# q's rotation in three engines instead of one: crosswise copies on ScalarE, the sine multiply on GpSimd

## The reference, cut to what matters

```
h = take(weight, ids)                                  # (8, 512, 256)
x = layernorm(h)
q, k, v = x @ w_aq, x @ w_ak, x @ w_av                 # 8 heads of 128
q, k = rope(q), rope(k)   # even*cos - odd*sin | even*sin + odd*cos over the halves of a head
s = q @ k.T / 128, causal;  p = softmax(s);  o = p @ v
h = h + o @ w_ao
h = h + moe(layernorm(h))                              # 8 experts, 1024 tokens each
```

## Time and profile before

| what | value |
|---|---|
| median of 3 runs | 1285.78 us (1285.78 to 1285.96) |
| the profiled execution: time, span | 1286.61 us, 1284.8 us |
| mean granted TensorE clock in it | 0.957 |
| busy: PE, DVE, ACT, POOL | 1148.5, 912.1, 609.5, 740.8 us |

### The profile page before, as it was taken

The page is one execution under the profiler, slowest core; times in us unless marked ns, Lnnn a source line. Parts: engine busy times, 40 slices in busy tenths (PEclk is TensorE's granted clock), DMA queues, the critical chain, the costliest instruction groups (busy, mean ns, idle before and its releaser), DMA issues. The chain is left out here.

```text
span 1284.8 us, 21944 instructions
## 1 busy us (share of the span) xinstructions
PE 1148.5 (89%) x7255; PEld 985.3 (77%) x7255; DVE 912.1 (71%) x1980; ACT 609.5 (47%) x1306; POOL 740.8 (58%) x783
## 2 busy tenths in 40 slices
PE   3899999999999999999999978015999999999995
PEld 2688888878878878878888863004999999999994
DVE  5888888898888998988988853775555555553522
ACT  4455545545555445545555543102654654655541
POOL 3776676776766776766766730005654744744425
PEclk9999999999999999999999998556999999999998
DMA  5000100100100100100100001304423623624212
GB/s 184 5 14 1 38 30 0 37 29 0 41 24 0 41 24 9 43 13 33 33 1 34 17 2 34 106 0 133 116 34 99 133 34 99 132 34 99 34 17 33
DMA packets 42170, 57.60 MB, mean 45 GB/s; under 512 B 8896, under 2 KB 34944, under 8 KB 41984
## 3 DMA queue, kind: packets, MB, share of 16 engines
q0 software_dynamic: 13824, 21.24, 9.2%
q1 hardware_dynamic: 28288, 35.58, 8.3%
HBM read 35.71 MB, written 16.91 MB: 41 GB/s over the span
## 5 line engine op out<-in xcount | busy, mean ns | idle before, releaser
L1125 DVE TENSOR_TENSOR hT_lo<-hid,hT_hi 128x512 fp32r<-128x512 f32 x128 | 89.4, 699 | 178.8 <-ACT hT_hi L1243 178.8
L268 ACT ACTIVATE prob<-bank,row_min 128x512 f32<-128x512 f32 (+3 forms) x256 | 136.1, 532 | 113.1 <-DVE row_min L389 113.0
L199 POOL TENSOR_SCALAR prob<-prob,row_inv 128x512 f32<-128x512 f32 (+3 forms) x256 | 135.0, 540 | 68.2 <-DVE row_inv L393 66.7
L1241 ACT ACTIVATE hid<-up,b_e 128x512 f32<-128x512 f32 x128 | 88.1, 688 | 154.8 <-PE up L1308 143.6
L339 DVE TENSOR_TENSOR pT_lo<-bank,pT_hi 128x384 fp32r<-128x384 f32 (+1 forms) x192 | 114.2, 595 | 50.8 <-ACT pT_hi L248 50.6
L949 POOL DMA_INDIRECT got<-routed_rows,tokens x64 | 85.8, 1341 | 102.7 <-DVE tokens L1119 85.4
L212 POOL TENSOR_TENSOR kT_lo<-k_cos,kT_hi 128x512 fp32r<-128x512 f32 x64 | 84.2, 1315 | 78.1 <-ACT kT_hi L248 78.1
L248 ACT ACTIVATE oT_hi<-bank 128x512 fp32r<-128x512 f32 x64 | 38.4, 599 | 186.5 <-PE bank L519 178.5
L206 POOL TENSOR_TENSOR q_cos<-q_cos,q_sin 128x512 f32<-128x512 f32 x64 | 82.3, 1287 | 55.1 <-DVE q_sin L376 55.0
L969 POOL DMA_INDIRECT out<-y,tokens x64 | 103.2, 1613 | 17.3 <-issue 14.8
L389 DVE TENSOR_REDUCE row_min<-bank 128x1 f32<-128x512 f32 (+3 forms) x256 | 112.4, 480 | 0.2
(11 more groups left out here) (196 smaller groups left out, 3855.8 us busy)
## 6 DMA issues: line engine op xcount, KB each, us to landing
raw<-in_w SPq DMA_DIRECT2D x16, 1024.0 KB, 8.1
emb_res<-emb SPq DMA_DIRECT2D x8, 512.0 KB, 3.7
out<-h SPq DMA_DIRECT2D x8, 512.0 KB, 2.9
routed_rows<-x SPq DMA_DIRECT2D x8, 512.0 KB
x<-in_wq SPq DMA_DIRECT2D x1, 1024.0 KB, 5.3
x<-in_wk SPq DMA_DIRECT2D x1, 1024.0 KB, 5.0
x<-in_wv SPq DMA_DIRECT2D x1, 1024.0 KB, 7.2
x<-in_wo SPq DMA_DIRECT2D x1, 1024.0 KB, 10.0
```

What stands on the lines that cost most here:

```text
L199: nc.gpsimd.tensor_scalar(pr, pr, row_inv[:, h % 2, k:k + 1], 1.0, ALU.mult, ALU.mult).then_inc(s["norm_done"], 1)
L268: nc.scalar.activation(prob[:, h % 2, col:col + w], s_ps[bk][:, pc:pc + w], ACT.Exp, bias=row_min[:, h % 2, k:k + 1], scale=-1.0, accum_ou ...
L1125: nc.vector.tensor_tensor(out, in_, hi.bitcast(F32), ALU.subtract)\
L1241: nc.scalar.activation(hid[:, t % 2, :], up_ps[t % 2][:], ACT.Gelu, bias=bias)
```

## The change

Three edits, all in attention:

1. For q, VectorE keeps only the cosine multiply (`mul_q`). ScalarE copies the two halves of the projection crosswise from PSUM into `q_sin` (`swap`), at the head of its slot, and GpSimd multiplies `q_sin` by the sine table before its add. Whatever waited for `q_rope` on TensorE now waits for `q_swap`. k's rotation stays.
2. On ScalarE, `qT_hi` moves behind `pT_hi` 0; on GpSimd, the add for k moves ahead of the low part of q.
3. In the start, the rounding of the output weight (`wo_hi`, 128x2048) moves from before slot 0 to slot 0, behind `kT_hi`.

```diff
             def add(b, h, x):
                 n = b * H + h
-                cos, sin = (q_cos, q_sin) if x == "q" else (k_cos, k_sin)
-                after(pool, f"{x}_rope", n + 1)
+                if x == "q":
+                    cos, sin = q_cos, q_sin
+                    after(pool, "q_swap", n + 1)
+                    nc.gpsimd.tensor_tensor(sin[:], sin[:], rope_q[:, 1, :], ALU.mult)\
+                        .then_inc(s["q_sin"], 1)
+                    after(pool, "q_sin", n + 1)
+                else:
+                    cos, sin = k_cos, k_sin
+                    after(pool, "k_rope", n + 1)
                 nc.gpsimd.tensor_tensor(cos[:], cos[:], sin[:], ALU.add).then_inc(s[f"{x}_add"], 1)
...
                     if live:
+                        add(b, h, "k")
                         low(b, h, "q")
-                        add(b, h, "k")
                         low(b, h, "k")
...
+            def swap(b, h):
+                n = b * H + h
+                after(act, "q_mul", n + 1)
+                after(act, "q_add", n)
+                nc.scalar.activation(q_sin[0:64, :], proj_ps[0][64:128, :], ACT.Copy)
+                nc.scalar.activation(q_sin[64:128, :], proj_ps[0][0:64, :], ACT.Copy)\
+                    .then_inc(s["q_swap"], 1)
...
-            act.wait_ge(s["wo_in"], 16)
-            hi_of(w_o[0][:], wraw_o, "w_hi")
...
+                    if live:
+                        swap(b, h)
                     if ok(h - 3):
                         after(act, "o_done", n - 3 + 1)
                         after(act, "out_done", n - 3)
                         hi_of(oT[0][:], o_ps[:], "o_hi")
+                    if ok(h - 2):
+                        t_high(b, h - 2, 0)
                     if live:
                         qk_high(b, h, "q")
-                    if ok(h - 2):
-                        t_high(b, h - 2, 0)
                     if ok(h - 1):
                         exp(b, h - 1, 0)
...
                     if live:
                         qk_high(b, h, "k")
+                    if isinstance(b, int) and b == 0 and h == 0:
+                        act.wait_ge(s["wo_in"], 16)
+                        hi_of(w_o[0][:], wraw_o, "w_hi")
...
-            def rope(b, h, x):
...
+            def mul_q(b, h):
+                n = b * H + h
+                after(dve, "q_proj", n + 1)
+                after(dve, "q_lo", n)
+                nc.vector.tensor_tensor(q_cos[:], proj_ps[0][:], rope_q[:, 0, :], ALU.mult)\
+                    .then_inc(s["q_mul"], 1)
...
                 for kt in range(KT):
-                    after(pe, "k_rope" if kt else "q_rope", b * H)
+                    after(pe, "k_rope" if kt else "q_swap", b * H)
...
-                after(pe, "k_rope" if i else "q_rope", n + 1)
+                after(pe, "k_rope" if i else "q_swap", n + 1)
```

More of the change, by code:

```diff
@@ L89, in build_attention @@
             ids_in emb_in res_in stats_done aggr_done var_eps rstd_done xn_ready xt_tr xt_hi xt_lo
-            q_proj k_proj v_proj q_rope k_rope q_add k_add q_hi k_hi q_lo k_lo v_hi v_lo
+            q_proj k_proj v_proj q_mul q_swap q_sin k_rope q_add k_add q_hi k_hi q_lo k_lo v_hi v_lo
             s_done s_min exp_done inv_done norm_done t_done t_hi t_lo o_done o_hi o_lo
@@ L366, in xt, with turn_k @@
                     low_of(xT[1][:, kt, :], proj_ps[kt][:], xT[0][:, kt, :], "xt_lo")
-            def rope(b, h, x):
+            def mul_q(b, h):
                 n = b * H + h
[L370 to L377, removed]
+                after(dve, "q_proj", n + 1)
+                after(dve, "q_lo", n)
+                nc.vector.tensor_tensor(q_cos[:], proj_ps[0][:], rope_q[:, 0, :], ALU.mult)\
+                    .then_inc(s["q_mul"], 1)
+            def turn_k(b, h):
+                n = b * H + h
+                ps = proj_ps[1]
+                after(dve, "k_proj", n + 1)
+                after(dve, "k_lo", n)
+                nc.vector.tensor_tensor(k_cos[:], ps[:], rope_k[:, 0, :], ALU.mult)
+                nc.vector.tensor_tensor(k_sin[0:64, :], ps[64:128, :], rope_k[0:64, 1, :], ALU.mult)
+                nc.vector.tensor_tensor(k_sin[64:128, :], ps[0:64, :], rope_k[64:128, 1, :], ALU.mult)\
+                    .then_inc(s["k_rope"], 1)
             def t_low(b, h, f):
@@ L456, in body @@
                     if live:
-                        rope(b, h, "q")
+                        mul_q(b, h)
                     if ok(h - 2):
@@ L461, in body @@
                     if live:
-                        rope(b, h, "k")
+                        turn_k(b, h)
                     if ok(h - 3):
```

## The result

The changed kernel takes 1279.79 us (median of 5 runs, 1279.59 to 1280.40) against 1285.96 for the kernel before on the same chip (5 runs, 1285.78 to 1286.48): a ratio of 0.9952, interval 0.9938 to 0.9967. That is 6.2 us off where I had forecast 14.7; the time lies inside the range, at its upper end. What follows answers two questions: where the other 8.5 us went, and which of the edits the 6.2 come from.

The account below looks back on a forecast made before the run. PE, busy 1148.5 of 1284.8 us, bounds most slots; its remaining waits come from late VectorE. Terms 4.3 + 7.7 + 1.0 + 1.0 + 0.7 = 14.7 us off 1285.78 give 1271.1, range 1261 to 1280.

Parts of the forecast that it names:

- the sum above would stand: Port lock between GpSimd's multiply and VectorE's `normalise`, `normalise2`: at most part of a dearer multiply; forecast total of 14.7 us unchanged.
- The two reordered lines do just that and cost nothing. Value: 0.: Ordinary slot: reordering on ScalarE and GpSimd covers q's later rotation, costs nothing and gains 0.
- Slot 6, 4.3: Slot 6 of six loop batches falls to 10.94 us through VectorE's relief: 6 x 0.71 = 4.3 us.
- Slot 7, 7.7: Loop's slot 7 falls from 13.42 to 12.13 us, `q_cos` starting at T7 + 4.4: six batches, 7.7 us.
- From its start to the reciprocal lie 3.53 us: Slot 5: `v_lo` starts about 9.25 us after the slot's first q projection (T5); the reciprocal follows 3.53 later.
- Clock, 1.0: TensorE's clock drop behind slot 7's first wait, in two batches, goes: 2 x 0.51 = 1.0 us.
- Batch 0's slot 7, 1.0: Slot 7 of batch 0 falls from 12.50 to 11.53 us: 1.0 us gained.
- The start, +0.7: Slots 0 to 2 of batch 0: moving `wo_hi` and starting slots 1 and 2 sooner gains 0.7 us, from 0 to 1.6.
- Prices: Durations taken for the moved work: GpSimd's multiply 1.29 us, between 0.8 and 2.88; ScalarE's two copies 1.05, between 0.6 and 1.3.
- second rival: Only slot 6 and little else gained, with copies at 1.3 and a multiply near 1.9 us: 1280, chance 0.15.
- The main case: Slot 7: no wait before the second transposes, one released by `xT_lo`, slot near 12.1 us; chance 0.62.
- The sign against it: TensorE's `turn` 0 waiting on `norm`, listed among the observations that would show the forecast wrong.

Follow-up runs that it names:

- the relief: Kernel before, old order, without q's two sine multiplies on VectorE and nothing in their place (GpSimd adds `q_cos` to itself): 1268.15 us, 0.9871.
- the narrow add: Changed kernel with GpSimd's add for k cut to 8 of 512 columns in slot 5 only: 1274.33 us, 0.9917.
- the order alone: Kernel before with both order edits, on ScalarE and GpSimd, and nothing of the split rotation: 1279.36 us, 0.9937.
- GpSimd's order alone: Kernel before with only the add for k moved ahead of the low part of q on GpSimd: 1288.95 us, 1.0017.

## Why the prediction was wrong

By slots, the forecast misses 8.7 us: 3.6 in the loop's slot 7, 2.3 in the start, 2.1 in the loop's slot 5, and 0.7 in small terms. The step that failed behind the first (in the main) and the third is a term that I put at nothing: `normalise2` behind a fuller GpSimd, with which "the sum above would stand". It takes 2.70 us instead of 0.96. Behind the second it is TensorE's clock in the start, also put at nothing. A further step failed without moving the number, by giving the gain to the wrong edit. Step by step:

- **"The two reordered lines do just that and cost nothing. Value: 0."** This step failed. They are worth 6.9 us by themselves (1279.36), after 1.4 that GpSimd's costs in the start, and without them the split costs 55 (1342.57). I priced them only in an ordinary slot of the changed kernel, where cover was there, and never asked what stood behind `qT_hi` in the slots where VectorE is late. The idle 0.83 of VectorE before `pT_lo` was in the trace of before.
- **Slot 6, 4.3.** Measured 4.1, but the order edits give it without any relief, as the relief gives it without them.
- **Slot 7, 7.7.** Measured 4.1: the slot ends at 12.73 instead of 12.13. From `q_cos` to `xT_hi` it is 5.94 us where I summed 5.8, and from there 1.96 as forecast. The rest is the start of the chain, `q_cos` at T7 + 4.8 and not 4.4: the reciprocal came at T6 + 2.3 and not 1.85, `rsqrt` and `normalise` followed (T7 + 2.9, not 2.45). Most of the lateness comes from slot 5, whose `normalise2` at 2.70 held up `v_lo`; with the narrow add there, slot 5 is back at 10.94, the reciprocal at T6 + 2.0, `q_cos` at T7 + 4.6 and slot 7 at 12.47.
- **"From its start to the reciprocal lie 3.53 us"; `v_lo` at T5 + 9.25.** Failed: `v_hi` was there at T5 + 9.3, but `v_lo` started at T5 + 10.6, behind `normalise2`. The 3.53 came out as 3.02, since the second pair met less of GpSimd (1.10 us instead of 1.61), which made good for 0.5 of it. This also gave slot 5 its 2.1 us of loss, which my sum had at 0. The Trainium skill, page SBUF — State Buffer, section "SBUF: two separate sides", had the rule for it; I named it and `normalise2`, then wrote that "the sum above would stand". The trace agrees with the rule, 2.70 against 0.96, and the sum did not stand. I had the right suspect and gave it no price. I had also looked only at the multiply: what `normalise2` met was the add for k and the low part of q behind it, and the loser was VectorE.
- **Clock, 1.0.** As forecast in the loop; the drops in batch 0 were not in the sum.
- **Batch 0's slot 7, 1.0.** Measured 0.85, 11.65 against 11.53. Without `normalise2` the chain was right to 0.12.
- **The start, +0.7.** Failed: it lost 1.6, 1.5 of it in slot 1. Slot 1 does start 0.4 sooner, but the wait for `v_lo` ahead of it is 2.09 us (1.41 before, and 1.41 without the multiply, so it is q's detour), and the clock drop behind that wait, which I had at nothing, costs 1.56 in slot 1's projection. `wo_lo` takes 3.39 and not 2.28, but slot 2 is only 0.25 longer (10.82 against 10.57). The move of `wo_hi` was harmless but bought nothing (1282.12 with it undone).
- **Prices.** Multiply 1.28 (taken 1.29); copies 0.59 each, 1.2 for the pair (taken 1.05). The unknowns that I had bounded with most care were not the ones that failed.

The main case's picture of slot 7 holds in its last wait, released by `xT_lo`, and in the first one gone. A second wait, 0.66, was not in it: `turn` 1 on the fourth `norm`. The sign against it that I had listed, a wait of `turn` 0 on `norm`, did not come. But slot 5 went above 10.94, which I had listed too. A slip of the sum in the second rival, 5 x 0.6 - 1.8 = 1.2 and not 1.25, changes nothing. That the time fell inside the range is luck: the range reached up to 1280 for a rival that wanted a multiply near 1.9 us, and the multiply took 1.28.

Against the order alone the split costs 0.45 us in each loop batch (91.10 against 90.66), and saves 0.8 in batch 0's slot 7. As a whole nothing can be told from zero: 0.9952 and 0.9937, with intervals that overlap. The loop loses at GpSimd what VectorE's relief gives.

## What to carry to other kernels

Before taking work off a late engine, look for the instruction it idles on and at what is queued ahead of that on the releasing engine; swapping two pairs of lines bought here all of what the change bought, and the 80 us of moved work added nothing. Try such swaps together when one wait passes through two queues, since neither alone shortened the kernel. Moving work to GpSimd can cost more than its own duration if it closes the gaps into which VectorE's SBUF-to-SBUF instructions fell (a multiply of 1.28 a slot cost 2.2 in each loop batch, all of it in slots 5 to 7), and here it was best put only into the stretches where VectorE is late, here one slot in eight.

## What the runs showed of the hardware

- VectorE's `normalise2`, with one tensor input in SBUF and its output in SBUF, waits out the GpSimd instruction beside it. Where GpSimd then leaves a gap, the pair ends 0.47 to 0.51 us behind it in every kernel of the table, and a pair takes 0.96 to 2.70 us. Work that reads PSUM keeps its time: `v_lo` 0.68 with `kT_lo` running on GpSimd.
- The one that starts first wins, and the other pays for all of it. Before, `wo_lo` started first: 2.28, and `kT_lo` 2.88. After, `kT_lo` started 0.04 us before it: `kT_lo` 1.28, `wo_lo` 3.39. That is 1.1 more on VectorE for a winner of 1.28.
- The same idle time is not always followed by the same clock. Behind waits of 2.09 and 2.07 us at the end of slot 0 it fell to 0.50, the lower of TensorE's two levels, in both kernels, but with the first matmul in one and 0.7 us later in the other. Behind the wait of 1.43 us in the loop's slot 7 of the kernel before it fell in two batches of six, and behind 1.41 to 1.43 in none of six with GpSimd's order alone. The profile of one execution does not tell which it will be in another.
- A half-height copy from PSUM on ScalarE, 64 x 512, takes 0.59 us, as one of 128 x 512 does.
